# A two-layer transformer kernel: rounds alternate between batches, and the next round's first norm, projections and maxima are placed beside the feed-forward

## The reference

```
for layer in (L0, L1):
    h = layernorm(x) * g1 + b1
    x = x + attention(h, h) @ wo1 + bo1            # 1024 x 1024 scores per head, softmax
    h = layernorm(x) * g2 + b2
    x = x + attention(h, context) @ wo2 + bo2      # 1024 x 77 scores per head
    h = layernorm(x) * g3 + b3
    a, gate = split(h @ w_ff1 + b_ff1)             # 2 x 1024 columns
    x = x + (a * gelu(gate)) @ w_ff2 + b_ff2
```

## Time and profile before

| | us |
|---|---|
| median of 3 runs | 2436.41 (2434.92 to 2436.89) |
| profiled execution | 2436.33 |
| its span | 2434.6 |
| PE busy | 2183.5 |
| DVE busy | 1747.9 |
| ACT busy | 1477.4 |
| POOL busy | 1158.5 |

### The profile page before, as it was taken

How to read it: one execution, slowest core, us unless ns; L and a number is a source line. 1 busy time by engine, 2 the same in 40 slices (tenths; PEclk the granted TensorE clock), 3 DMA queues, 4 the chain that set the end, 5 groups by cost and what they waited for, 6 DMA issues and landing times.

```text
span 2434.6 us, 59106 instructions
## 1 busy us (share of the span) xinstructions
PE 2183.5 (90%) x25392; PEld 1447.4 (59%) x25392; DVE 1747.9 (72%) x3148; ACT 1477.4 (61%) x1948; POOL 1158.5 (48%) x730
## 2 busy tenths in 40 slices
PE   4999998899799999899959999989996999998998
PEld 1566665675356666567525666656753666666675
DVE  6888886555588888565558888865556888885664
ACT  2788787234288888633328888772333787885342
POOL 4667656122176675522217676552222666654231
PEclk8999999999799999999969999999998999999999
DMA  3222220000131231000023223100001212210000
GB/s 85 68 69 51 76 60 26 1 19 16 33 88 50 58 88 41 25 8 12 16 68 81 57 58 82 47 25 1 19 16 46 75 49 70 76 35 19 10 10 18
DMA packets 52437, 106.62 MB, mean 44 GB/s; under 512 B 9552, under 2 KB 13648, under 8 KB 52176
## 3 DMA queue, kind: packets, MB, share of 16 engines
q1 hardware_dynamic: 52176, 102.84, 15.9%
HBM read 50.25 MB, written 2.10 MB: 21 GB/s over the span
## 4 chain that ended last, share of the span: by engine, by line
PE 63%; DVE 19%; ACT 9%; issue 4%; DMA 2%; POOL 1%; SPq 1%; POOLq 0%; DVEq 0%; ACTq 0%
PE scores L689 7%; PE scores L691 7%; PE scores L690 7%; PE work L770 7%; PE scores L797 6%; PE scores L790 6%; DVE minima L1306 6%; DVE prob L1321 4%; PE work L689 3%; PE work L690 3%; PE work L691 3%; ACT prob L1123 3%; PE work L819 3%; PE work L815 3%; PE work L817 3%
## 5 line engine op out<-in xcount | busy, mean ns | idle before, releaser
L637 POOL TENSOR_TENSOR prob<-prob 128x1024 f16<-128x1024 f32 x256 | 582.7, 2276 | 554.2 <-ACT prob L1124 543.4
L1306 DVE TENSOR_REDUCE minima<-work 128x1 f32<-128x512 f32 x1024 | 681.5, 683 | 52.4 <-PE work L770 36.4
L1123 ACT ACTIVATE prob<-scores 128x1024 f32<-128x1024 f32 x512 | 526.0, 1027 | 125.2 <-PE scores L797 108.2
L1124 ACT ACTIVATE prob<-scores 128x1024 f16<-128x1024 f32 x512 | 523.0, 1021 | 0.0
L815 PE MATMUL work<-vals,prob 128*128 128x65 f16 x4096 | 430.1, 193 | 15.5 <-POOL prob L637 13.3
L819 PE MATMUL work<-vals,prob 128*128 128x65 f16 x4096 | 430.6, 196 | 0.0
L817 PE MATMUL work<-vals,prob 128*128 128x64 f16 x4096 | 430.5, 193 | 0.0
L815 PEld LDWEIGHTS work<-vals,prob 128*128 128x128 f16 x4096 | 383.8, 99 | 77.7 <-POOL prob L637 14.9
L770 PE MATMUL work<-ka,qa 128*128 128x512 f16 x1024 | 402.0, 396 | 25.3 <-DMA kb<-staged_k 16.1
L817 PEld LDWEIGHTS work<-vals,prob 128*128 128x128 f16 x4096 | 380.7, 97 | 58.1
L819 PEld LDWEIGHTS work<-vals,prob 128*128 128x128 f16 x4096 | 381.2, 97 | 0.0
(11 more groups left out here) (166 smaller groups left out, 4469.8 us busy)
## 6 DMA issues: line engine op xcount, KB each, us to landing
qa<-staged_q SPq DMA_DIRECT2D x128, 128.0 KB, 2.4
ka<-staged_k SPq DMA_DIRECT2D x128, 128.0 KB, 2.4
raw_even<-in_pairs SPq DMA_DIRECT2D x32, 384.0 KB, 3.4
raw_odd<-in_pairs SPq DMA_DIRECT2D x32, 384.0 KB, 3.3
raw_odd<-in_pieces SPq DMA_DIRECT2D x20, 512.0 KB, 3.6
raw_even<-in_pieces SPq DMA_DIRECT2D x20, 512.0 KB, 3.7
qb<-staged_q SPq DMA_DIRECT2D x64, 128.0 KB, 2.4
kb<-staged_k SPq DMA_DIRECT2D x64, 128.0 KB, 2.4
```

The lines of the kernel that those rows point to most:

```text
L637: pool.tensor_tensor(prob[1][:, slot, :], prob32[:, slot, :], prob[0][:, slot, :], ALU.subtract).then_inc(a.polished, 1)
L1123: act.activation(prob32[:, n % RING, :], source, ACT.Exp)
L1124: act.activation(prob[0][:, n % RING, :], source, ACT.Exp)\
L1306: dve.tensor_reduce(minima[:, t, h:h + 1], out[:, :], AX.X, ALU.max, negate=True)\
```

## The change

The rounds now run batch 0 layer 0, batch 1 layer 0, batch 0 layer 1, batch 1 layer 1 (`l = g // BATCH`, batch `g % BATCH`), so that a round's input is ready before the round ahead of it ends. `end_round` is gone, and with it the drains and the meeting of the engines.

The input of the next round's first norm is loaded into `x_next`, half of the probability buffer, which the feed-forward leaves free; `moments` and `normalise` of that norm read it there. x itself is stored at the end of each round and loaded again in head pair 1 of the next; the addition of the bias row 0 moves from the end of the first norm to head pair 6, since x isn't there before. `params` holds both layers and is loaded once.

`up` and `down` are one function `feed_forward(g, ahead)`. `ahead` walks the next round's list of steps up to a named mark. In `up`: moments at units 2 to 5, normalise at 6, 7, 11, 12, transposes after units 8, 9, 14, 15, ACT's part at units 8 to 11 and behind unit 15, splits at 11, 12 and in `down`; q0 after unit 13, k0 after unit 14. In `down`: q1 and k1 after projection 1, v0 after 2, v1 after 3, and four of the 16 maxima after each of projections 4 to 7. The banks change so that these fit: q0, v0 in `work[1]`, k0, v1 in `work[3]`, the next norm's transposes in `work[0]` and `work[2]`, the projections of `down` in `four[2]` and `four[3]`. `down` waits for the product of unit 14 before it starts, where it waited for that of unit 15. The first norm of round 0 also has x in both places, and its DMAs are in another order.

```diff
 def self_steps():
+    q, k, v = queries(0, 0), key_blocks(0, 0), values(0, 0)
     out = [Step("start", 0, 0, 0, 0)]
-    out += taken(queries(0, 0) + key_blocks(0, 0) + values(0, 0))
-    out += [Step("split", ("S", 1), 0, 0, 0)]
-    out += sum(maxima(0, 0), []) + [Step("shift", 0, 0, 0, 0)] + maxima(0, 1)[0]
+    for name, part in (("q0", q[:1]), ("k0", k[:1]), ("q1 k1", q[1:] + k[1:]), ("v0", v[:1])):
+        out += taken(part) + [mark(name)]
+    out += taken(v[1:]) + [Step("split", ("S", 1), 0, 0, 0), mark("v1")]
+    for n, tile in enumerate(maxima(0, 0)):
+        out += tile + [mark(f"max{n}")]
+    out += [Step("shift", 0, 0, 0, 0)] + maxima(0, 1)[0]
...
         @block.sync
+                pace.walk(do, "max0")
+                if g:
+                    store(g - 1)
                 pace.walk(do)
...
+            for g in range(ROUNDS):
+                attention(g)
+                for n in (8, 9):
+                    fetch(g, "W", n)
+                if g + 1 < ROUNDS:
+                    hold(sp, y_full, g * (3 * TILES) + TILES + 1)
+                    load_next(g + 1)
+                for n in (6, 7):
+                    fetch(g, "W", n)
...
         @block.tensor
+                    elif ahead and n in (8, 9):
+                        turn(index + 1, n - 8)
+                    elif ahead and n == 13:
+                        ahead("q0")
+                    elif ahead and n == 14:
+                        ahead("k0")
+                        turn(index + 1, 2)
+                    elif ahead and n == 15:
+                        turn(index + 1, 3)
+                marks = {1: ["q1 k1"], 2: ["v0"], 3: ["v1"], 4: ["max0", "max1"], 5: ["max2", "max3"],
+                         6: ["max4", "max5"], 7: ["max6", "max7"]}
                 for t in range(TILES):
-                    if t == 0:
-                        pe.wait_ge(inner_ready, (g + 1) * (BLKS * FF_CHUNKS) + 2)
-                    project(g * 3 + 2, t, 6)
+                    if t == 0:
+                        pe.wait_ge(inner_ready, base + BLKS * FF_CHUNKS + 1)
+                    project(index, t, 6)
+                    if ahead:
+                        for name in marks.get(t, []):
+                            ahead(name)
-                end_round(pe, g)
...
         @block.vector
             def moments(index, p):
+                source = x if index % 3 else x_next
...
+                for t in range(TILES):
+                    if ahead and t < 2:
+                        split(index + 1, t + 2)
+                    take_y(index, t)
+                    if ahead:
+                        for name in marks.get(t, []):
+                            ahead(name)
```

More of the change, by code:

```diff
@@ L202, in self_unit @@
             loads[3].append(Step("split", ("W", pair), par, 0, 0))
+        elif pair == 6:
+            loads[3].append(Step("bias", 0, par, 0, 0))
+        if pair == 1:
+            loads[0].append(Step("reload", 0, par, 0, 0))
         loads[6].append(Step("fetch", ("C", pair + 1), par, 0, 0))
@@ L257, in __init__, with walk @@
         self.passed = collections.Counter()
-    def walk(self, do):
-        units = 0
-        at = 0
-        for s in STEPS:
+        self.next = self.units = self.at = 0
+    def walk(self, do, until=None):
+        while self.next < len(STEPS):
+            s = STEPS[self.next]
+            self.next += 1
+            if s.kind == "mark":
+                if s.step == until:
+                    return
+                continue
             if s.kind == "unit":
                 self.unit = s.par, s.head
-                at, units = units // 2, units + 1
-            do(s, at + s.ahead)
+                self.at, self.units = self.units // 2, self.units + 1
+            do(s, self.at + s.ahead)
             self.passed[s.kind] += 1
@@ L317, in build @@
         self_high = work[1]
-        first_high = four[2:4] + four[0:2] + [work[1]]
+        first_high = [work[1], work[3], four[0], four[1], work[1], work[3]]
         x_outs = [work[3], work[2], work[1]]
@@ L324, in high_bank, with turn_bank, y_bank @@
         def high_bank(n):
-            return first_high[n % len(first_high)] if n <= len(first_high) else self_high
+            return first_high[n] if n < len(first_high) else self_high
+        def turn_bank(index, p):
+            return work[2] if index % 3 == 0 and p % 2 else work[p % 2]
+        def y_bank(index, t):
+            return four[t % 2 + (2 if index % 3 == 2 else 0)][:, 0:DIM]
         def peak_bank(k):
@@ L547, in _ @@
+            store(ROUNDS - 1)
+            sp.wait_ge(x_stored, ROUNDS * 16 + CREDIT)
         @block.gpsimd
@@ L664, in _ @@
             pool.sem_inc(bias_added, CREDIT)
+            for p in range(GROUPS):
+                norm(0, p)
             for g in range(ROUNDS):
-                for p in range(GROUPS):
-                    norm(g * 3, p)
-                pool.wait_ge(params_loaded, (g + 1) * 32)
-                add_bias(g * 3, 0)
                 attention(g)
@@ L676, in _ @@
                 add_bias(g * 3 + 2, 2)
+                if g + 1 < ROUNDS:
+                    for p in range(GROUPS):
+                        norm(g * 3 + 3, p)
                 hold(pool, xscores_full, (g + 1) * X_ALL)
@@ L718, in do @@
                     elif step.kind in ("q", "k"):
-                        if pace.here("start") == 1 and step.kind == "q":
+                        if pace.here("start") == 1:
                             pe.wait_ge(norm_split, g * 3 * GROUPS + 2 * (s + 1))
@@ L782, in do @@
                             pe.wait_ge(a.work_free, pace.n(*HIGH) + HIGH_RING)
+                        elif pace.here("score") == 1 and g:
+                            pe.wait_ge(y_free, g * (3 * TILES) + 2)
                         pe.wait_ge(a.exp_done, pace.n("score") + 1)
@@ L829, in do @@
                         last.then_inc(a.work_full, 1)
-                pace.walk(do)
+                return lambda until=None: pace.walk(do, until)
             def project(index, t, w, merges=None):
-                out = four[t % 2][:, 0:DIM]
+                out = y_bank(index, t)
                 pe.wait_ge(y_free, index * TILES + (t + 1))
@@ new lines, in _ @@
+            hold(dve, next_loaded, 16)
+            for p in range(GROUPS + 2):
+                if p < GROUPS:
+                    moments(0, p)
+                if 1 <= p <= GROUPS:
+                    normalise(0, p - 1)
+                if p >= 2:
+                    split(0, p - 2)
+            hold(dve, params_loaded, 16)
+            walk = attention(0)
+            for g in range(ROUNDS):
+                walk()
+                dve.wait_ge(bias_added, g * 3 + (1 + CREDIT))
+                cross(g)
+                walk = attention(g + 1) if g + 1 < ROUNDS else None
+                feed_forward(g, walk)
```

220 lines of the change are left out of this document (125 added, 95 removed).

## The result

The changed kernel takes 2363.09 us (median of 4 runs, 2356.96 to 2367.88) against 2436.39 us of the kernel before (4 runs, 2434.92 to 2436.89). The ratio is 0.9706, 95% interval 0.9682 to 0.973: 3% faster. The forecast was 2362, with a range of 2349 to 2384.

A forecast was written before the change was run, and what follows sets the result against it. Bound by PE inside a round and by latency at three boundaries. Profiled span 2434.6 - 73 (boundaries) - 1.8 (last wait) - 4 (first units) - 3 (start) + 3 (up) + 5 (pair 6) = 2360.8; forecast 2362 us, range 2349 to 2384.

The forecast's parts named there:

- The boundary: Last up matmul to copy of the next round's first row of shifts: three take 126 us instead of 199, -73.
- E: End of the last up matmul in a round, the zero from which the boundary's times are counted.
- That DVE sets the pace there with PE: From projection 4 on, two banks make PE wait for DVE's reductions: 4.8 us per projection with four maxima.
- Up: Up part grows 3.9 us by q0, k0 and transposes, plus 1 a round for POOL stalling DVE's norm work.
- Pair 6: Bias row 0 on POOL (4.53 us) holds up DVE's refine: 1.3 a round, +5 us; bounds 0 and 18.
- Start: Program start: ACT needs `params` alone, no longer waits for `rows`: -3 us, between -6 and +3.
- Last wait and the DMAs: Wait of 1.77 ahead of round 3's down part goes, -1.8; store and loads cost 0, at worst 2 a boundary.
- The first unit: First unit behind a boundary runs at full clock: -4 us for three boundaries; 0 if clock drops, -8 if all slower.
- The main rival: PE's clock falls inside the feed-forward: 2434 us, no change, or 2509 if already in up; 5%.
- hidden work not free: POOL locks and hand-offs in up and pair 6 take their upper bounds, +23.5: 2386 us; 18%.
- Nothing collides: Both POOL terms 0, whole first unit faster, start at its bound: 2347 us; 10%.
- SP late: Copies of q1 and k1 reach PE 5 us late in the down part, +10: 2372 us; 7%.

The follow-up runs named there:

- k4: Changed kernel with two of each projection's four maxima moved inside projections 4 to 7, two left behind each: 2343.46 us, ratio 0.9625.
- k3: Changed kernel with all 16 maxima behind the last projection of the feed-forward: 2365.6 us, ratio 0.9715.
- k2: Changed kernel with the first attention's bias row added in four pieces over head pair 6: 2353.3 us, ratio 0.9666.
- k11: k7 with POOL's bias additions behind a round's second and third norm also in four pieces each: 2340.19 us, ratio 0.9599.
- k8: Changed kernel with idle matmuls on PE, four ahead of the transposed shifts and six ahead of the first score: 2355.85 us, ratio 0.9674.
- k9: Changed kernel with only the norm beside the feed-forward; next round's projections and maxima behind the last projection: 2382.18 us, ratio 0.9772.
- k7: Changed kernel with maxima inside and behind projections 4 to 7 and first bias row in four pieces: 2336.25 us (again 2336.72).

## Why the prediction was right

The time was 2363.09 for a forecast of 2362, and the case that came is the likeliest one. By its steps:

- *The boundary*, E + 38.0: measured 37.53 to 37.58. The steps inside hold too. The first addition to x is at E + 4.70, PE waits 0.92 ahead of q1 (0.9 predicted), and projections with their maxima are 4.72 apart (4.8). The copies of the keys are there when PE comes to the maxima at E + 19.7, without a wait.
- *That DVE sets the pace there with PE*: shown by k4, where the same work in another order takes 3.49 a projection. The prediction had the period right, and did not see that it is hardly shorter than the projection and the reductions one after the other, as k3 shows.
- *Up*: 3.9 + 1 predicted, 5.23 measured. From start to start, q0 and k0 take 1.29 each and the three groups of transposes 0.44, 0.65 and 0.44, in all 4.1. Another 0.9 is one unit beside POOL's weight splits, whose 12 matmuls take 3.51 and not 2.59: PE waits 0.76 behind it for the normalise, and that took 2.17 for two tiles, where 0.73 is usual. A low part beside the splits took 2.04 instead of 0.68. This is the place that the term named. No run moved the splits, so that POOL is the cause here is argued from the rows. The wait behind the bias row is not part of the growth, since it was there before.

```profile
579.87 0.66 PE L917 MATMUL work<-ident,xn 128*128 128x128 f32 x4 [0.76 <-DVE xn L1439]
```

```profile
577.64 2.17 DVE L1439 TENSOR_SCALAR xn<-prob,mean_var,rstd 128x256 f32<-128x256 f32 x2
```

- *Pair 6*: 1.3 a round predicted, 1.0 to 1.2 measured in three of four rounds of the trace, 2.0 in the other, of which 0.78 is a wait for the row of shifts (4.4 in the ledger, since one of the same four pairs before was 46.40); k2 takes it away. One refine stood for 3.54 instead of 1.22 behind the 4.53 on POOL, and more than half of that was covered. The Trainium skill's rule (SBUF — State Buffer, section Who interferes with whom) is borne out by this row and by k2 and k11: the refine ends at 931.54, 1.08 behind POOL's end at 930.46, as if it had done its 1.22 only then. It would have misled only if the standing time had been taken for the kernel's loss: 2.3 on DVE were 1.1 in the pair.
- *Start*: -3 predicted, -4.3 measured. The wait for `rows` is gone; ACT's first high part starts at 18.48.
- *Last wait and the DMAs*: -1.9, and no first score waits longer for the row of shifts because of the store.
- *The first unit* is the step that failed. I had -4 from the clock and wrote "0 if the clock drops in the gap"; it does drop there, and the trace has +1.5, of which +1.7 is round 0's and the three boundaries are even with before. The prediction took it that full clock up to the maxima lasts through the unit; the clock fell around the row of shifts instead, where PE waits 1.10 ahead of the transposed shifts and 1.50 ahead of the first score. k8 shows that PE's gaps there are the cause: with them filled the three take 68.2, 6.0 less than before and more than the -4 reckoned. Which of the two fillings does it isn't shown. Where the clock fell at a boundary, in every trace but k9's it did so between 1.6 us ahead of the copy and 1.7 behind it, so ahead of the wait of 1.50, which begins over 3 us behind the copy; the order in time speaks for the first gap and the loose stretch of maxima ahead of it. The main rival, the clock falling already in the down part or in up, did not happen: PEclk is 1.00 in up with three groups of transposes more, and 0.99 to the copy. Only in the last microsecond ahead of the first boundary's copy is it at half.
- *Not accounted for*: 2.7 in the ledger, in two places. The steady pairs other than pair 6 hold 0.9 of it. Most pairs take 45.56, but in both kernels single ones take 0.5 to 1.0 more, each time in another place, and in these PE waits ahead of a score for the DMA of the row of shifts: by the pages 3.8 in all before and 5.2 after, and between 0.8 (k3) and 5.2 in the traces here. The first pair of round 3 took 46.54, where 44.88 is usual: the clock was at half at its start.

```profile
757.83 0.39 PE L861 MATMUL scores<-qb,kb 128*128 128x512 f16 x1 [0.64 <-DMA qb<-shift_rows]
```

```profile
1828.30:1831.70 3.40, 3.40 (x19) 1.85 (x18) 1.46 (x5) 0.96 (x2) 0.10 (x1) 0.51 0.02 5
```

  The stretches from the last unit to the first product of up hold the other 1.8: 630.4 for four rounds before, 632.2 after. In the first two, 1.1 and 2.2 longer, PEclk is 0.96, where it was 0.97. That this makes the difference isn't shown, nor why a row of shifts is late.

The rivals: *hidden work not free* had the right two places and bounds far too high. *Nothing collides* is refuted by k2. *SP late* did not occur.

That the two numbers meet is in part luck: the span was to be 2360.8, the profiled execution had 2366.2, and the median of four runs lies between. The first units were off by 5.5 and the rest by 2.7, against 2.7 that the boundaries and the start gave more than reckoned.

## What to carry to other kernels

Reckon a boundary from the last matmul that nothing in it can change, walk both engines through the new order with durations of the rows, and look at what each waits for after the move: here two engines handed four tiles to each other in turn, and interleaving at a finer grain gave 4.5 us a boundary where placing work side by side had given almost nothing. A long POOL instruction beside DVE's two-input ones is cheaper in pieces between DVE's own work than in one. And after a change that closes gaps, look at the granted clock in what follows them: a kernel can gain in one place and give it back in the next stretch, so read the clock's windows before a step is judged by its total.

## What the runs showed of the hardware

- A first unit of 22.7 us at PEclk 1.00 took up to 27.2 at lower ones (0.78 over it in k3), and the same kernel shows it at other boundaries in another execution. Ten matmuls of 512 columns, whose product goes unused, in gaps of 1.1 and 1.5 us removed it at all 12 boundaries traced; a boundary was 0.08 longer with them (37.61 against 37.53, k8).
- 16 reductions of 128 x 512, each behind a matmul, take 9.65 us at full clock (k3) and 11.04 at half (k9, and before): DVE's pace in such a pair is set in part by PE's clock.
- A sum of the bias row in four pieces takes POOL 5.41 in all instead of 4.53 (k11), and the kernel's part there is still shorter.
- A DMA of one row of shifts, which is usually there in time, kept PE waiting for 0.4 to 0.9 us in single pairs: 1.1 us in all in one execution (the second trace of k7) and 4.5 in another of the same kernel.
